# Linear attention and gated FFN on one core: attention transposed by DMA instead of TensorE, with a new order of queries and projections

## The reference

```python
xn = layernorm(x)                                  # x: 8 x 1024 x 256
q, k, v = xn @ Wq.T, xn @ Wk.T, xn @ Wv.T          # 16 heads of 16
q = elu(q) + 1;  k = elu(k) + 1
kv_state = einsum('bhnd,bhne->bhde', k, v);  k_state = k.sum(2)
attn = einsum('bhnd,bhde->bhne', q, kv_state) / max(q . k_state, 1e-6)
local = 3-tap convolution of xn along the tokens, per channel, + conv_b
attention = (attn + local) @ Wp.T + bp
ffn = (silu(xn @ wg.T) * (xn @ wu.T)) @ wd.T       # hidden 768, int weights / 127
out = x + attention + ffn
```

## Time and profile before

| | |
|---|---|
| three runs, median (lowest to highest) | 511.0 us (510.78 to 511.91) |
| the profiled run, its time | 511.35 us |
| its span | 509.7 us |
| busy in the span: TensorE, VectorE, ScalarE, GpSimd | 493.8, 431.9, 334.4, 143.6 us |
| the chain that ended last: TensorE, VectorE, ScalarE | 86%, 7%, 2% |
| mean granted clock of TensorE | 0.997 |
| DMA | 45.36 MB, 89 GB/s |

### The profile page before, as it was taken

One profiled execution on the slowest core, in us unless ns is written; L12 is line 12 of the kernel. 1 busy time (PEld: TensorE's weight loads), 2 busy tenths in 40 slices (PEclk: granted clock), 3 DMA queues, 4 the chain that ended last, 5 costly groups with the idle time before them and its releaser, 6 DMA issues.

```text
span 509.7 us, 11017 instructions
## 1 busy us (share of the span) xinstructions
PE 493.8 (97%) x3968; PEld 304.9 (60%) x3968; DVE 431.9 (85%) x833; ACT 334.4 (66%) x522; POOL 143.6 (28%) x152
## 2 busy tenths in 40 slices
PE   7889979999999999999999999999999999999997
PEld 6536445565747556574755657566564756657576
DVE  4889888988888888888888888888988889897787
ACT  2666856748566775856667585766748577674770
POOL 4554414050131404114140421415032140501050
PEclk9998999999999999999999999999999999999999
DMA  8534524232523334253242424423352442233012
GB/s 301 184 57 83 111 42 116 52 125 42 164 46 84 103 57 133 41 136 69 53 132 41 144 41 125 80 48 119 52 152 41 107 99 41 84 46 80 3 41 84
DMA packets 68653, 45.36 MB, mean 89 GB/s; under 512 B 33424, under 2 KB 68112, under 8 KB 68624
## 3 DMA queue, kind: packets, MB, share of 16 engines
q1 hardware_dynamic: 59360, 35.79, 24.8%
q0 software_dynamic: 8448, 8.39, 11.1%
q10 hardware_dynamic: 816, 0.79, 0.4%
HBM read 20.32 MB, written 8.39 MB: 56 GB/s over the span
## 4 chain that ended last, share of the span: by engine, by line
PE 86%; DVE 7%; ACT 2%; issue 2%; DMA 2%; ACTq 0%; DVEq 0%
PE ps L1197 16%; PE ps L1034 15%; PE ps L1206 15%; PE ps L1216 15%; PE ps L1140 14%; PE ps L1096 5%; PE ps L1105 3%; PE ps L1159 2%; DMA wv_raw<-in_L_attn_Wv_dram 2%; DVE maxima L663 1%; DVE hl L900 1%; DVE hid L894 1%; ACT act_g L536 1%; DVE local L830 1%; DVE power L656 0%
## 5 line engine op out<-in xcount | busy, mean ns | idle before, releaser
L536 ACT ACTIVATE act_g<-ps,scales 128x512 f32<-128x512 f32 x96 | 66.0, 687 | 45.5 <-PE ps L1206 43.4
L894 DVE SCALAR_TENSOR_TENSOR hid<-act_g,scales,ps 128x512 f32<-128x512 f32 x96 | 71.5, 745 | 23.9 <-ACT act_g L536 23.6
L900 DVE TENSOR_TENSOR hl<-hid,hh 128x512 f16<-128x512 f32 x96 | 68.3, 713 | 1.7 <-ACT hh L544 0.4
L361 POOL TENSOR_TENSOR xT<-xh,xl 128x1024 f32<-128x1024 f16 x15 | 31.8, 2121 | 109.1 <-issue 109.1
L544 ACT ACTIVATE hh<-hid 128x512 f16<-128x512 f32 x96 | 59.6, 622 | 4.4 <-DVE hid L894 4.4
L1197 PE MATMUL ps<-xh,g_wh 128*128 128x512 f16 x192 | 57.6, 381 | 1.9 <-ACT u_wh L455 1.4
L1206 PE MATMUL ps<-xl,g_wh 128*128 128x512 f16 x192 | 57.1, 379 | 0.0
L1206 PE MATMUL ps<-xl,u_wh 128*128 128x512 f16 x192 | 57.1, 379 | 0.0
L1197 PE MATMUL ps<-xh,u_wh 128*128 128x512 f16 x192 | 57.1, 379 | 0.0
L499 ACT ACTIVATE k_neg<-ps,scales 128x512 f32<-128x512 f32 x30 | 20.6, 688 | 53.1 <-PE ps L1140 53.1
L326 POOL TENSOR_SCALAR xn<-x_in,neg_mean,rstd 128x256 f32<-128x256 f32 x62 | 50.6, 829 | 4.3 <-POOL rstd L333 4.2
(11 more groups left out here) (149 smaller groups left out, 966.8 us busy)
## 6 DMA issues: line engine op xcount, KB each, us to landing
xb<-bp_sb SPq DMA_DIRECT2D x16, 512.0 KB, 3.3
xb<-in_L_attn_x_dram POOLq DMA_DIRECT2D x16, 512.0 KB, 5.9
x_in<-in_L_attn_x_dram SPq DMA_DIRECT2D x15, 512.0 KB, 4.1
out_dram<-out_sb SPq DMA_DIRECT2D x14, 512.0 KB, 2.9
out_dram<-out_sb SPq DMA_DIRECT2D x4, 256.0 KB, 2.1
wg_int<-in_L_ffn_w_gate_dram SPq DMA_DIRECT2D x1, 768.0 KB, 7.8
wu_int<-in_L_ffn_w_up_dram SPq DMA_DIRECT2D x1, 768.0 KB, 9.3
wd_int<-in_L_ffn_w_down_dram SPq DMA_DIRECT2D x1, 768.0 KB, 11.8
```

The costliest lines, as they stand in the source:

```text
L536: nc.scalar.activation(act_g[:, j % 2, :], ps[:, gate_bank(j), :], ACT.Silu, scale=silu_in).then_inc(silu_ready, 1)
L894: nc.vector.scalar_tensor_tensor(out=hid[:, j % 2, :], in0=act_g[:, j % 2, :], scalar=h_mul, in1=ps[:, gate_bank(j) + 1, :], op0=ALU.mult, ...
L900: nc.vector.tensor_tensor(hl[:, j, :], hid[:, j % 2, :], hh[:, j, :], ALU.subtract).then_inc(hl_ready, 1)
```

## The change

The transposes of `attn` leave TensorE in all steps that attend, but for the two chunks that the last step attends to in addition. ScalarE makes a float16 high half of the scaled attention (`attn_high`), VectorE the low half (`attn_low`), SyncE turns both by DMA (`turn_attn`), GpSimd adds the turned halves into `y` (`begin_y`), and VectorE adds `local` (`put_y`). In the steady steps TensorE's order becomes k/v(0), k/v(1), queries, accumulate(0), gate/up(0) and (1), accumulate(1), project_q (banks 4, 5 now), gate/up(2) to (5), project_y(0), down(0), project_y(1), down(1). Both ReLUs of the queries move to ScalarE, behind `hidden_high(1)` (`query_evict`, Q_SPLIT = 2); their exponential and `put_q` run in the next step. `attn_high(0)` stands between `key_parts(0)` and `key_parts(1)`. `down` takes the high halves of j = 5 behind the low halves of j = 0 to 3. VectorE's and ScalarE's orders change with it. In step (0,0) the last weight scales move behind the FFN. The diff, twelve columns of indentation left out:

```diff
-D_SPLIT = 4
+D_SPLIT = 3
 X_SPLIT = 4
-FIRST_X_SPLIT = 2
-Y_SPLIT = (2, 3)
-Y_PROJECT = 4
+Y_SPLIT = (4, 5)
+Q_SPLIT = 2
...
+        attn_h = sb("attn_h", [P, TILES, D], F16)
+        attn_l = sb("attn_l", [P, TILES, D], F16)
+        aT_h = sb("aT_h", [P, TILES, KT, P], F16)
+        aT_l = sb("aT_l", [P, TILES, KT, P], F16)
...
+def turn_attn(b, c):
+    if not (isinstance(b, int) and b == 0 and c == 0):
+        sp.wait_ge(y_begun, at(b, c, 2, 0))
+        sp.sem_inc(turns_due, 1)
+    turn([(attn_h, aT_h, attn_h_ready, ah_turned), (attn_l, aT_l, attn_l_ready, al_turned)],
+         at(b, c, 2, 2), lambda channels: channels[:, :, :, :])
...
+    if attend:
+        turn_attn(b - 1, c)
     if ahead:
         turn_x(*((b, 1) if c == 0 else (b + 1, 0)))
...
+def begin_y(b, c, p):
+    tiles, cols = slice(2 * p, 2 * p + 2), slice(p * PAIR, (p + 1) * PAIR)
+    pool.wait_ge(ah_turned, at(b, c, 16, 16))
+    pool.wait_ge(al_turned, at(b, c, 16, 16))
+    if not (isinstance(b, int) and b == 0 and c == 0):
+        pool.wait_ge(yl_ready, at(b, c, 2, p - 1))
+    nc.gpsimd.tensor_tensor(y[:, :, cols].rearrange("p k (i t) -> p i k t", i=2), aT_h[:, tiles, :, :],
+                            aT_l[:, tiles, :, :], ALU.add).then_inc(y_begun, 1)
...
+    if attend:
+        begin_y(b - 1, c, 0)
+        begin_y(b - 1, c, 1)
+    if ahead:
...
+def attn_high(b, c, p):
+    act.wait_ge(attn_ready, at(b, c, 2, p + 1))
+    if p == 0 and not (isinstance(b, int) and b == 0 and c == 0):
+        act.wait_ge(ah_turned, at(b, c, 16, 0))
+    tiles = slice(2 * p, 2 * p + 2)
+    nc.scalar.activation(attn_h[:, tiles, :], attn[:, tiles, :], ACT.Copy,
+                         scale=attn_to_y).then_inc(attn_h_ready, 1)
...
-    def query_parts():
+    def query_evict():
         act.wait_ge(q_done, at(b, c, 1, 1))
...
+        nc.scalar.activation(q_neg[:, :, :], ps[:, Q_BANK:Q_BANK + 2, :], ACT.Relu,
                              scale=q_flip).then_inc(q_flipped, 1)
+        nc.scalar.activation(q_relu[:, :, :], ps[:, Q_BANK:Q_BANK + 2, :], ACT.Relu,
+                             scale=q_down).then_inc(q_read, 1)
+    def query_exp(b, c):
         act.wait_ge(q_flipped, at(b, c, 1, 1))
+        if not (isinstance(b, int) and b == 0 and c == 0):
...
+        query_exp(*((b, 0) if c == 1 else (b - 1, 1)))
     key_parts(0)
+    if attend:
+        attn_high(b - 1, c, 0)
     key_parts(1)
-    if past:
-        query_parts()
-    else:
+    if attend:
+        attn_high(b - 1, c, 1)
+    if not ahead:
+        query_evict()
+        query_exp(b, c)
...
-        if j == J - 1 and past and not attend:
+        if j == 2 and past and not attend:
             high(p_w[0][:, :, :], w_raw["p"][:, :, :], "p", p_hi)
         if j >= 1:
             hidden_high(j - 1)
+        if past and ahead and j == Q_SPLIT:
+            query_evict()
+        if j in (0, 1) and not past:
+            x_high(0, 1, (j,))
         if j == D_SPLIT and not past:
             high(d_w[0][:, :, :], ffn_raw["d"][:, :].rearrange("p (k n) -> p k n", k=J), "d", d_hi)
-        if attend and j == (Y_SPLIT[0] if ahead else 0):
+        if attend and j == (3 if ahead else 2):
             y_high(b - 1, c, 0)
-        if attend and j == (Y_SPLIT[1] if ahead else 1):
+        if attend and j == (4 if ahead else 2):
             y_high(b - 1, c, 1)
-        if ahead and j == (X_SPLIT if attend else FIRST_X_SPLIT):
+        if past and ahead and j == X_SPLIT:
             x_high(*((b, 1) if c == 0 else (b + 1, 0)))
...
+    if not past:
+        query_evict()
...
-def put_y(b, c, p, banks):
+def attn_low(b, c, p):
+    dve.wait_ge(attn_h_ready, at(b, c, 2, p + 1))
+    if p == 0 and not (isinstance(b, int) and b == 0 and c == 0):
+        dve.wait_ge(al_turned, at(b, c, 16, 0))
+    tiles = slice(2 * p, 2 * p + 2)
+    nc.vector.scalar_tensor_tensor(out=attn_l[:, tiles, :], in0=attn[:, tiles, :], scalar=attn_to_y,
+                                   in1=attn_h[:, tiles, :], op0=ALU.mult,
+                                   op1=ALU.subtract).then_inc(attn_l_ready, 1)
...
+def put_y(b, c, p):
     cols = slice(p * PAIR, (p + 1) * PAIR)
-    dve.wait_ge(yT_done, at(b, c, 2, p + 1))
+    dve.wait_ge(y_begun, at(b, c, 2, p + 1))
     if p == 0:
         dve.wait_ge(conv_done, at(b, c, KT, KT))
     if not (isinstance(b, int) and b == 0 and c == 0):
-        dve.wait_ge(yl_ready, at(b, c, 2, p - 1))
         dve.wait_ge(wp_done, at(b, c, 2, p - 1))
+    nc.vector.tensor_tensor(y[:, :, cols], y[:, :, cols], local_of(c, p), ALU.add).then_inc(y_ready, 1)
...
         hidden(4)
         hidden_low(3)
-        across(3)
         hidden(5)
         hidden_low(4)
         hidden_low(5)
+        down_low_half()
+        across(3)
         attention_scales()
         low(kv_w[1][:, :, 0:D], w_raw["k"][:, :, :], "k", kv_w[0][:, :, 0:D], k_hi, 1, kv_lo)
         low(kv_w[1][:, :, D:2 * D], w_raw["v"][:, :, :], "v", kv_w[0][:, :, D:2 * D], v_hi, 1, kv_lo)
-        down_low_half()
         put_res(0, DOWN)
         put_res(1, DOWN)
...
+    if ahead:
+        stats(nb, ncx)
     tap(pb, pc, 0, 0)
     tap(pb, pc, 1, 0)
-    if ahead:
-        stats(nb, ncx)
+    put_q(pb, pc)
+    put_k(0)
     if attend:
         normalise(b - 1, c, 0, QKV)
         normalise(b - 1, c, 1, QKV)
-    put_k(0)
-    tap(pb, pc, 0, 2)
-    tap(pb, pc, 1, 2)
     put_k(1)
-    relu_q()
     if attend:
-        put_y(b - 1, c, 0, TURNED)
-        put_y(b - 1, c, 1, TURNED)
+        attn_low(b - 1, c, 0)
+    else:
+        tap(pb, pc, 0, 2)
+        tap(pb, pc, 1, 2)
     if ahead:
         for j in range(J):
             hidden(j)
-            if j == 0:
-                put_q()
+            if attend and j == 0:
+                attn_low(b - 1, c, 1)
+                tap(pb, pc, 0, 2)
+                tap(pb, pc, 1, 2)
             if j >= 1:
                 hidden_low(j - 1)
+            if attend and j == 2:
+                put_y(b - 1, c, 0)
+            if attend and j == 3:
+                put_y(b - 1, c, 1)
             if attend and j == Y_SPLIT[0]:
                 y_low(b - 1, c, 0)
-            if attend and j == Y_SPLIT[1]:
-                y_low(b - 1, c, 1)
-            if j == (X_SPLIT if attend else FIRST_X_SPLIT):
+            if j == X_SPLIT:
                 x_low(nb, ncx, 0)
                 x_low(nb, ncx, 1)
-            if j == 3 and not attend:
+            if j == 4 and not attend:
                 projection_scales()
         hidden_low(J - 1)
+        if attend:
+            y_low(b - 1, c, 1)
...
         hidden(0)
-        y_low(b - 1, c, 0)
+        attn_low(b - 1, c, 1)
+        tap(pb, pc, 0, 2)
+        tap(pb, pc, 1, 2)
         hidden(1)
         hidden_low(0)
-        y_low(b - 1, c, 1)
         put_state()
+        put_y(b - 1, c, 0)
+        put_y(b - 1, c, 1)
         hidden(2)
         hidden_low(1)
+        y_low(b - 1, c, 0)
+        y_low(b - 1, c, 1)
         output(b - 1, c, 0, WP)
...
-        put_q()
+        put_q(b, c)
...
-        if past:
-            pe.wait_ge(v_ready, at(b, c, 2, 1))
+        if attend:
+            pe.wait_ge(attn_ready, at(b - 1, c, 2, 1))
+        elif past:
...
@@ -1182,12 +1260,9 @@
         if j == 0:
             pe.wait_ge(v_ready, at(b, c, 2, 2))
-        elif j == 1 and not past:
-            pe.wait_ge(v_ready, 1)
         elif j == 1:
-            pe.wait_ge(q_read, at(b, c, 1, 1))
+            pe.wait_ge(v_ready, at(b, c, 2, 1))
         else:
             pe.wait_ge(hid_ready, at(b, c, J, j - 1))
...
-        for j in range(J):
+        def high_half(j):
             if p == 0:
                 pe.wait_ge(hh_ready, at(b, c, J, j + 1))
             both(hh, d_w[0], j, start=(j == 0))
+        def low_half(j):
+            if p == 0:
+                pe.wait_ge(hl_ready, at(b, c, J, j + 1))
+            return both(hl, d_w[0], j, stop=(j == J - 1))
+        for j in range(J - 1):
+            high_half(j)
+        for j in range(J - 2):
+            low_half(j)
+        high_half(J - 1)
         with pe.If(is_wide["down"]):
             pe.wait_ge(d_lo, 1)
             for j in range(J):
                 both(hh, d_w[1], j)
-        for j in range(J):
-            if p == 0:
-                pe.wait_ge(hl_ready, at(b, c, J, j + 1))
-            ins = both(hl, d_w[0], j, stop=(j == J - 1))
+        for j in range(J - 2, J):
+            ins = low_half(j)
         ins.then_inc(down_done, 1)
...
+        gate_up(5)
         turn_maxima(3)
-        gate_up(5)
-        spread_maxima(3)
+        pe.wait_ge(hid_ready, J - 1)
...
         down(0, DOWN)
+        spread_maxima(3)
         down(1, DOWN)
...
     project_kv(0)
-    if attend:
...
+    pe.wait_ge(res_ready, at(b, c - 1, 2, 2))
+    pe.wait_ge(acc_kept, at(b, c, 1, 0))
+    pe.wait_ge(q_read, at(b, c - 1, 1, 1))
+    if not ahead:
         query(b - 1, c, 0, QKV)
         query(b - 1, c, 1, QKV)
-    project_kv(1)
-    project_q()
-    accumulate(0)
-    if attend:
```

(29 more changed lines are left out.)

95 lines of the change are left out of this document (51 added, 44 removed).

## The result

The changed kernel takes 581.75 us (median of 4 runs, 581.31 to 582.48) where the kernel before takes 510.99 (510.78 to 511.91): ratio 1.138, 95% interval 1.136 to 1.140. It is slower, as forecast, but by 71 us and not by 92: the forecast was 603. The time is that of rival B (582), but not for rival B's reason: the clock did fall, and terms of both signs cancel (see the sum in the part on the prediction).

The account below looks back on a forecast made before the run. TensorE, busy 97%, was taken to bound the kernel. 511.35 + 60.3 (steady steps, transposes' saving included) + 9.3 (last step) + 1 (first two) + 21 (clock) = 603 us; range 562 to 632, holding 0.84.

Parts of the forecast that it names:

- rival B: Whole kernel: same four waits a step, but the clock holds, 582 us; chance 0.24.
- Bound and sign: Whole kernel: TensorE's work is a step's price, removing transposes saves 1.03 a step, new waits exceed it; slower, chance 0.95.
- The four waits: Steady step, TensorE: accumulate(0) 1.97, gate/up(0) 0.70, gate/up(5) 1.57, project_y(0) 1.43; step 34.58, +60.3 us over 13 steps.
- the fourth: Steady step: project_y(0) waits 1.43 us for y_low(0), starting at 26.5 when gate/up(5) was over at 25.1.
- Hidden work: Steady step: attention's DMA transfers and GpSimd's two adds cost nothing; adds end at 20.3, put_y(0) due at 20.5.
- one number on a later transfer: Steady step: a transfer 1.5 us later would push hidden(3) by 1.3, but silu(3) holds that until 22.5 anyway.
- The sentence that allowed at most 0.3 a step: Steady step: GpSimd's adds beside VectorE lie where VectorE has a gap, costing 0, at most 0.3 us a step.
- The clock: Steady steps: thin TensorE stretches drop its clock once a step, 1.6 x 13 = +21 us; bounds none and +42.
- The first two steps: Opening: 2.5 us of idle gone, but late low weights delay k/v(0) and the third wait comes; +1, bounds -3 and +3.
- the third wait: gate/up(5) waits 1.57 us a steady step for hidden(3), behind ScalarE's two query evictions; expected in the second step too.
- The last step: Last step: project_y(0) starts 25.9 after the step's start instead of 16.7, +9.3 us; bounds 4 and 11.
- A: Whole kernel, the forecast itself: four waits a step and one fall of the clock, 603 us; chance 0.45.

Follow-up runs that it names:

- every kernel with a better order: Changed kernel with project_q directly behind the queries: 563.95 us; DMA turning with TensorE's queries and project_q placed as before: 527.05; that with put_y later: 513.78.
- all shifted: Changed kernel with two spare GpSimd fills at the start, so everything behind runs later: 583.80 us (2 runs).
- gap 0.6 longer: Changed kernel with ScalarE's first fp16 copy of the attention done twice, in front of the second key/value eviction: 598.23 us, ratio 1.170.
- the opening tried alone: Kernel before with only the first step's changes of the change: 509.48 us, ratio 0.997.
- the fastest kernel here: Kernel before with the opening's changes, first query features added by VectorE, second step's chunk and projection-weight conversions moved: 506.39 us, ratio 0.991.

## Why the prediction was right and where it was wrong

**Bound and sign: right.** TensorE was the price of a step, the 1.03 of transposes was the only saving, and the waits exceed it.

**The four waits: right, in place and size.** Predicted 1.97, 0.70, 1.57, 1.43, in all 5.67; measured between starts 1.99, 0.86, 1.37, 1.43, in all 5.65. Walking one step through the new queues with distances between starts gave the chain too: gate/up(5) at 23.35 predicted and 23.37 found, project_y(0) at 26.5 and 26.53. Steps without a fall take 34.4 against 34.58. Each wait was tied to its cause by one edit: v_sb by the copy's place, attn by project_q's place, hid by the query evictions' place; the fourth, for yl, only moved with the others and was not taken away alone.

**Hidden work: right for this kernel, wrong as a margin.** The adds end when the prediction said (20.4), and cutting them changes the equal steps by nothing. But the prediction put one number on a later transfer (1.5 us later would push hidden(3), and silu(3) covers it) and none on everything else coming earlier; that case came up in every kernel with a better order. There the wait is 1.05 and the stretching of one instruction 0.95. The sentence that allowed at most 0.3 a step for GpSimd beside VectorE was worked out from 1.63 less 1.34, a duration less a distance between starts; like with like it is 1.63 - 1.43 = 0.20. It holds nearly, and costs nothing, only because beside the adds VectorE has just hidden(2), which is not slowed (0.75), and the start of hidden_low(1), 0.82 instead of 0.68 (up to 1.10 in other steps). What it is in general stands at the end.

**The clock: the term that was mis-sized.** "One fall a step, 1.6 x 13 = +21" was 3 falls of 1.6, +4.9: the size of one fall was right (35.93 - 34.31 = 1.6), their number was not. The step read from one fall in the trace of before, and from one step in which it held, that each thinner stretch must bring one. The traced runs with such a stretch show 3 of 13 (the changed kernel, the copy moved, the last step on TensorE, the adds cut, all shifted), 7 (query evictions earlier, with the same stretch) and 7 (gap 0.6 longer), and not in the same steps; project_q in front of the wait, which fills the stretch, leaves none. That is -16 us against the forecast, three quarters of its error. The bounds (none to two a step) held it.

**The first two steps: wrong sign.** +1 predicted, -3.5 found. The 2.5 us of waits in the first step went as estimated (46.25 to 43.65, -2.6), but the step that would give them back does not. The cost that the prediction named, k/v(0) waiting for low weights that come later, is real: it is the 1.02 of the opening tried alone. Not seen was that the change takes away what makes them late, GpSimd's add of the first query features beside VectorE's scales, and that its add into xT no longer lies beside hidden_low at the end of the second step (3.22 above). The second step takes 27.98 instead of 28.86, although the third wait came there too (1.81).

**The last step: near.** +9.3 predicted, +10.9 found. project_y(0) stands at 25.7 after the step's start (549.59 - 523.91), predicted 25.9. The price was off by the clock: during the wait of 7.28 it fell, and project_y(0), 1.31 elsewhere, takes 2.54 (to 552.13 in order of time), the gate/up part behind it 2.38 instead of 1.73: +1.9, and 9.0 + 1.9 = 10.9. Turning that chunk by TensorE gives 9.9 back.

**Sum.** Clock -16.1, first steps -4.5, waits -2.2 (58.1 instead of 60.3), last step +1.6: -21.2 against 603, which is 581.8. That this is rival B's number is luck: B had the clock hold, and against its 582 the falls (+4.9) and the last step (+1.6) are cancelled by the first steps (-4.5) and the waits (-2.2). The forecast's chance for B (0.24) was too low against 0.45 for A: one occurrence and one counter-example in the trace gave no reason to prefer "in each step".

## What to carry to other kernels

An engine that is 97% busy gains nothing from losing 1 us of work if the new order puts one round trip through two other engines in front of its next instruction: walk one step by distances between starts before counting the saving, and keep independent work (here project_q) behind each such round trip. Price work held for hidden at the place where it would lie after the order improves too. A small GpSimd add can hold VectorE for its whole length, so put it where VectorE has nothing the critical engine waits for: from 509.5 to 506.4 us, the last step of the way to the fastest kernel here, was moving such adds and what stood beside them.
